# First layer norm by ScalarE's square root and one Newton step; GELU split on ScalarE; matmuls and loads reordered at the border and in the last slot

## The reference

```python
xn = _layernorm(x, axis=-1)              # (x - m) / sqrt(v + 1e-5)
...
local_out = _full_attention(x, local_qkv_w, scale)
sparse_out = _sparse_global_attention(x, sparse_qkv_w, scale)   # keeps the 102 largest scores of a row
mem_out = _memory_head(x, memory_bank, memory_proj_w, mem_out_w, mem_out_b)
pred_out = _prediction_head(x, ...)      # two linear layers, exact GELU, a third layer
...
return combined @ warboss_w + warboss_b
...
g = _silu(_L0_ffn_ref(xn, ...))          # relu(xn @ w1 + b1) @ w2 + b2, width 2048
x = x + s * g
```

## Time and profile before

| | |
|---|---|
| Time, median of 3 runs | 2529.58 us (2529.27 to 2530.76) |
| The profiled execution: its own time | 2529.44 us |
| The profiled execution: span from the first to the last instruction | 2527.6 us |
| PE busy | 2515.6 us |
| PEld busy | 2120.0 us |
| DVE busy | 2291.1 us |
| ACT busy | 1299.4 us |
| POOL busy | 1151.8 us |
| DMA | 551.74 MB, mean 218 GB/s |

### The profile page before, as it was taken

How to read it: one execution, slowest core, us unless ns; L and a number is a source line. 1 busy time by engine, 2 the same in 40 slices (tenths; PEclk the granted TensorE clock), 3 DMA queues, 4 the chain that set the end, 5 groups by cost and what they waited for, 6 DMA issues and landing times.

```text
span 2527.6 us, 36088 instructions
## 1 busy us (share of the span) xinstructions
PE 2515.6 (100%) x12432; PEld 2120.0 (84%) x12432; DVE 2291.1 (91%) x5184; ACT 1299.4 (51%) x2128; POOL 1151.8 (46%) x975
## 2 busy tenths in 40 slices
PE   9999999999999999999999999999999999999999
PEld 8888888878888888888888888888888888888887
DVE  7566556999999999999999999999999999999995
ACT  5666666644444444444544444444444444444443
POOL 2544444533444444444444444444444444444444
PEclk9999999999999999999999999999999999999999
DMA  8888888964655565546554665466556654665443
GB/s 262 331 309 314 309 311 326 340 230 138 236 197 200 167 234 200 200 167 233 200 200 166 224 206 197 166 219 214 200 167 216 215 199 164 216 217 199 165 157 122
DMA packets 166149, 551.74 MB, mean 218 GB/s; under 512 B 17936, under 2 KB 32976, under 8 KB 157648
## 3 DMA queue, kind: packets, MB, share of 16 engines
q1 hardware_dynamic: 165680, 548.90, 61.9%
q10 hardware_dynamic: 288, 0.52, 0.1%
HBM read 415.15 MB, written 134.22 MB: 217 GB/s over the span
## 4 chain that ended last, share of the span: by engine, by line
PE 95%; DVE 4%; ACT 0%; issue 0%; POOL 0%; POOLq 0%; ACTq 0%
PE acc L74 9%; PE acc L76 9%; PE acc L75 9%; PE hid L76 9%; PE hid L74 9%; PE hid L75 9%; PE ps L74 5%; PE ps L76 5%; PE ps L75 5%; PE o L1709 4%; PE scores L1696 4%; PE o L1713 2%; PE scores L74 2%; PE scores L76 2%; PE scores L75 2%; PE o L75 2%
## 5 line engine op out<-in xcount | busy, mean ns | idle before, releaser
L1428 POOL TENSOR_TENSOR h_lo<-h,h_hi 128x512 fp32r<-128x512 f32 x254 | 336.0, 1323 | 719.7 <-ACT h_hi L1323 718.2
L1561 DVE MAX8 ranks<-early 128x8 f32<-128x512 f32 x819 | 564.7, 689 | 13.0
L1581 DVE MATCH_REPLACE8 early<-ranks,early 128x512 f32<-128x512 f32 x756 | 511.1, 676 | 0.0
L1322 ACT ACTIVATE h<-hid,small 128x512 f32<-128x512 f32 x255 | 175.7, 689 | 479.9 <-PE hid L76 479.8
L74 PE MATMUL acc<-w,h_hi 128*128 128x512 f32 x1016 | 408.0, 402 | 0.0
L76 PE MATMUL hid<-xnT,w 128*128 128x512 f32 x1020 | 397.5, 390 | 0.0
L74 PE MATMUL hid<-xnT,w 128*128 128x512 f32 x1020 | 397.0, 389 | 0.0
L75 PE MATMUL hid<-xnT,w 128*128 128x512 f32 x1020 | 396.8, 389 | 0.0
L76 PE MATMUL acc<-w,h_lo 128*128 128x512 f32 x1016 | 396.5, 390 | 0.0
L75 PE MATMUL acc<-w,h_hi 128*128 128x512 f32 x1016 | 396.5, 390 | 0.0
L1428 POOL TENSOR_TENSOR pT_s<-pT,pT_s 128x512 fp32r<-128x512 f32 x256 | 327.2, 1300 | 42.2 <-ACT pT_s L1337 42.2
(11 more groups left out here) (237 smaller groups left out, 5170.2 us busy)
## 6 DMA issues: line engine op xcount, KB each, us to landing
w<-ffn_scratch SPq DMA_DIRECT2D x512, 512.0 KB, 4.1
xnT_scratch<-xnT SPq DMA_DIRECT2D x16, 2048.0 KB, 13.7
kv_scratch<-kv_out SPq DMA_DIRECT2D x32, 1024.0 KB, 6.1
tl<-tile_scratch SPq DMA_DIRECT2D x64, 512.0 KB, 4.0
tile_scratch<-tiles_out SPq DMA_DIRECT2D x15, 2048.0 KB, 8.5
xnT<-xnT_scratch SPq DMA_DIRECT2D x60, 512.0 KB, 7.1
ffn_scratch<-ffn SPq DMA_DIRECT2D x16, 1024.0 KB, 4.3
values<-kv_scratch SPq DMA_DIRECT2D x16, 1024.0 KB, 6.2
```

What stands on the lines that cost most here:

```text
L1322: nc.scalar.activation(h32[:, c % 2, :], src[:, :], ACT.Relu, bias=bias)
L1428: return nc.gpsimd.tensor_tensor(out_, value, hi_.bitcast(F32), ALU.subtract).then_inc(ready, 1)
L1561: l_step = count(nc.vector.max(top_l[:, own], larger[:, :]))
L1581: l_step = count(nc.vector.match_replace(larger[:, :], top_l[:, own], larger[:, :], LOWEST))
```

## The change

- **First layer norm.** For half 0, ACT computes the square root of var + eps (`ACT.Sqrt`) as soon as DVE has it, DVE takes its reciprocal and makes one Newton step instead of seed and three steps. The other halves are as before.
- **First projections.** All high parts of mp and pi come first (8 matmuls), then the 8 with the weights' low parts, which alone wait for `w_first`. ACT copies the weights of only one block of rows, not two, ahead of the transposed tokens. `WARM` is 48 instead of 60.
- **GELU, in every half.** ACT writes GELU back into the PSUM bank, waits for its own result, and copies the high part from there; DVE's cast is gone, and its two low parts (128x512 each) are taken from PSUM. The banks of p1a and p1b are free only when those are made.
- **Border.** On PE, `f2` of chunk 0 goes ahead of the local scores of slot 1, `f2` of chunk 1 ahead of the transposes behind them, and in slot 2 `f2` of chunk 4 ahead of the first transposes of the sparse head. `full_max` and `full_inverse` of slot 3 come one round earlier. SP loads w2's chunk 2 and w1's chunk 4 earlier.
- **Last slot.** The parts of `f2` for tile 0 are each moved ahead by one place.

The core of the diff:

```diff
-WARM = 60
+WARM = 48
...
+            act.wait_ge(ln_step, LN_VAR)
+            nc.scalar.activation(rstd[:, :], var[:, :], ACT.Sqrt).then_inc(deviation, 1)
             act.wait_ge(mp_in, 32)
             nc.scalar.activation(wp_hi[:, :, 0:2 * P], wp[:, :, 0:2 * P], ACT.Copy).then_inc(w_h, 1)
-            for k in (0, 1):
-                weights(k)
+            weights(0)
             for k in range(KT):
                 tokens(k)
-            for k in (2, 3):
+            for k in (1, 2, 3):
                 weights(k)
...
                             c = int(name == "p1b")
-                            last = nc.scalar.activation(gelu[:, c, :], src, ACT.Gelu, bias=b_p1[:, c:c + 1])
+                            nc.scalar.activation(src, src, ACT.Gelu, bias=b_p1[:, c:c + 1]).then_inc(gelu_step, 1)
+                            act.wait_ge(gelu_step, 2 * n + c + 1)
+                            last = nc.scalar.activation(gelu_hi[:, c, :], src, ACT.Copy)
...
-                link(nc.vector.tensor_scalar(rstd[:, :].bitcast(I32), var[:, :].bitcast(I32),
-                                             -0.5, RSQRT_SEED, ALU.mult, ALU.add))
-                link(nc.vector.tensor_scalar(var[:, :], var[:, :], -0.5, None, ALU.mult))
-                for _ in range(NEWTON):
+                if first(n):
+                    nc.vector.tensor_scalar(half_var[:, :], var[:, :], -0.5, None, ALU.mult)
+                    dve.wait_ge(deviation, 1)
+                    link(nc.vector.reciprocal(rstd[:, :], rstd[:, :]))
+                    var_scaled, steps = half_var, 1
...
-                    dve.wait_ge(bank_read, done(n, "p1b"))
-                    nc.vector.tensor_copy(gelu_hi[:, :, :], gelu[:, :, :]).then_inc(ghi_ready, 1)
-                    dve.wait_ge(ghi_ready, n + 1)
-                    subtract(gelu_lo[:, :, :], gelu[:, :, :], gelu_hi[:, :, :]).then_inc(lo_ready, 1)
+                    for c, name in enumerate(("p1a", "p1b")):
+                        dve.wait_ge(bank_read, done(n, name))
+                        subtract(gelu_lo[:, c, :], ps[:, bank(n, name), :], gelu_hi[:, c, :]).then_inc(lo_ready, 1)
...
+        FIRST_ROUNDS = {1: (1, 2), 3: (2, 3)}
...
-                r_max, r_inverse = (1, 2) if m == 1 else (R_MAX[T % HTILES], R_INVERSE[T % HTILES])
+                r_max, r_inverse = FIRST_ROUNDS.get(m, (R_MAX[T % HTILES], R_INVERSE[T % HTILES]))
...
                     load_kv(U_VL, 0)
+                    load_w2(2, 2)
                     load_tl(2, 2, 2)
-                    load_w2(2, 2)
+                    load_w1(4, 4)
                     load_w2(3, 3)
...
             transposes(2)
             f2(C, c, h, (0,))
             f1(C + 2, c + 2, h)
+            f2(C + 1, c + 1, h, (0,))
             pe.wait_ge(mix_ready, m - 2)
             head_out(g, U_VS)
             f1(C + 3, c + 3, h)
-            f2(C + 1, c + 1, h, (0,))
+            f2(C + 2, c + 2, h, (0,))
             pe.wait_ge(at_l, g + 1)
             mix(m - 2, (m - 2) % TL_RING)
-            for i in (2, 3):
-                f2(C + i, c + i, h, (0,))
+            f2(C + 3, c + 3, h, (0,))
```

More of the change, by code:

```diff
@@ L244, in stage1 @@
     CONSTS = 3
+    LN_VAR = 3
     with ExitStack() as ctx:
@@ L699, in layer_norm_parts @@
                 link(nc.vector.tensor_scalar(var[:, :], mv[:, :, 1], EPS, None, ALU.add))
-                link(nc.vector.tensor_scalar(rstd[:, :].bitcast(I32), var[:, :].bitcast(I32),
-                                             -0.5, RSQRT_SEED, ALU.mult, ALU.add))
-                link(nc.vector.tensor_scalar(var[:, :], var[:, :], -0.5, None, ALU.mult))
-                for _ in range(NEWTON):
+                if first(n):
[3 more added lines that the diff above has]
+                    var_scaled, steps = half_var, 1
+                else:
+                    link(nc.vector.tensor_scalar(rstd[:, :].bitcast(I32), var[:, :].bitcast(I32),
+                                                 -0.5, RSQRT_SEED, ALU.mult, ALU.add))
+                    link(nc.vector.tensor_scalar(var[:, :], var[:, :], -0.5, None, ALU.mult))
+                    var_scaled, steps = var, NEWTON
+                for _ in range(steps):
                     link(nc.vector.tensor_tensor(nt[:, :], rstd[:, :], rstd[:, :], ALU.mult))
-                    link(nc.vector.tensor_tensor(nt[:, :], nt[:, :], var[:, :], ALU.mult))
+                    link(nc.vector.tensor_tensor(nt[:, :], nt[:, :], var_scaled[:, :], ALU.mult))
                     link(nc.vector.scalar_tensor_tensor(out=rstd[:, :], in0=nt[:, :], scalar=1.5, in1=rstd[:, :],
@@ L920, in first_projections @@
                 dst = [ps[:, bank(0, name), :] for name in ("mp", "pi")]
+                pe.wait_ge(w_h, 1)
                 for k in range(KT):
                     pe.wait_ge(bank_read, k + 1)
-                    if k == 0:
-                        pe.wait_ge(w_first, 1)
                     for d, m in zip(dst, (MP, PI)):
-                        c = slice(m * P, (m + 1) * P)
-                        nc.tensor.matmul(d, wp_hi[:, k, c], xnT[:, 0, k, HI, :], start=k == 0, stop=False)
-                        nc.tensor.matmul(d, wp_lo[:, k, c], xnT[:, 0, k, HI, :], start=False, stop=False)
+                        nc.tensor.matmul(d, wp_hi[:, k, m * P:(m + 1) * P], xnT[:, 0, k, HI, :],
+                                         start=k == 0, stop=False)
+                pe.wait_ge(w_first, 1)
+                for d, m in zip(dst, (MP, PI)):
+                    for k in range(KT):
+                        nc.tensor.matmul(d, wp_lo[:, k, m * P:(m + 1) * P], xnT[:, 0, k, HI, :],
+                                         start=False, stop=False)
                 for d, m in zip(dst, (MP, PI)):
@@ L1280, in slot @@
                     finished()
-                load_w1(C + 4, c + 4)
+                if m > 1:
+                    load_w1(C + 4, c + 4)
                 if T == 0 and b < B:
@@ L1765, in slot @@
                 if T % 2 == 0:
+                    if m == 2:
+                        f2(C, c, h)
                     pe.wait_ge(pT_h, 4 * g + 2)
@@ L1769, in slot @@
                     transposes(2)
-                    f2(C, c, h)
+                    if m > 2:
+                        f2(C, c, h)
                     f1(C + 2, c + 2, h)
@@ L1787, in slot @@
                 else:
+                    if m == 1:
+                        f2(C, c, h)
                     pe.wait_ge(pT_h, 4 * g + 2)
                     head_scores(T % TL_RING, T_QL, U_KL, sl_done)
-                    f2(C, c, h)
+                    if m > 1:
+                        f2(C, c, h)
                     if not known_first(m, 2):
@@ L1796, in slot @@
                     f1(C + 2, c + 2, h)
+                    if m == 1:
+                        f2(C + 1, c + 1, h)
                     pe.wait_ge(pl_ready, m + 1)
                     transposes(0)
-                    f2(C + 1, c + 1, h)
+                    if m > 1:
+                        f2(C + 1, c + 1, h)
                     f1(C + 3, c + 3, h)
```

10 lines of the change are left out of this document (6 added, 4 removed).

## The result

The changed kernel takes 2534.80 us (median of 22 runs), the kernel before 2530.06 in the runs beside it: ratio 1.0017, 95% interval 1.0012 to 1.0023. That is 4.7 us more, where the forecast was 2.1 us above the profiled execution's time (2531.5 us) and 2533.8 was the upper end of the range. The sign and the class (within 0.2%) hold, the size doesn't. The profiled execution took 2534.98 us, its span is 2532.4, 4.8 more than before.

A forecast was written before the change was run, and what follows sets the result against it. PE was taken as the bound, so only its waits could be won. Half 0 +1.5, border +0.6, last slot 0: +2.1 on the profiled 2529.44 gives 2531.5 us; range 2528.3 to 2533.8, the forecast's own bounds 2529.7 to 2533.8.

The forecast's parts named there:

- First layer norm: Half 0, var + eps to scaling: 1.35 us instead of 2.38, a gain of 1.03 us (0.7 to 1.2).
- ACT's chain to mo: Half 0: start 1.03 us earlier, table load 1.28 and GELU pair 1.25 more; mo at 40.5 instead of 39.02.
- the rival with 1.4 us more for the switch: Table load ahead of Exp in half 0 takes 1.4 us longer than the trace's 1.28: 2532.9 us, chance 0.04.
- Waits 2.8 us: Half 0: PE waits 2.8 us ahead of mo, for the low part of wt.
- Half 0: Half 0 costs 1.5 us (1.0 to 2.2) instead of gaining 1.3, and all that follows is later by it.
- Halves 1 to 15: ACT has 1.25 us more work in each half, but 1.2 us remain ahead of p2: costed at nothing.
- Slot 1: Border: local scores 1.83 us later, PE waits 1.7 us for w2; the slot ends 1.2 us later than before.
- Slots 2 to 7: PE at +0.2 in slot 2, leaves slot 3's wait 0.7 us earlier, is 0.6 us later from slot 7 on.
- the border's term: Slots 1 to 7 together cost +0.6 us (-1.1 to +1.7); PE not waiting in slot 7 would fell it.
- Last slot: Wait of 0.4 us is covered, but the last f2 part needs POOL's last low part: nothing won or lost.
- the two terms: The costs of half 0, +1.5 us (1.0 to 2.2), and of the border, +0.6 us (-1.1 to +1.7).

The follow-up runs named there:

- e4: Changed kernel with 24 more transposes of the identity on PE ahead of mo in half 0, result unread: ratio 1.0012 to the kernel before, median 2533.06 us.
- e2: Changed kernel with the GELU path of the kernel before (GELU into SBUF, DVE makes high and low part): ratio 1.0008 to the kernel before, median 2532.06 us.
- e3: Changed kernel with one tiny Exp in half 0 while ACT waits for DVE's maximum, loading the table early: ratio 1.0009 to the kernel before, median 2532.57 us.
- e1: Changed kernel with the first layer norm of the kernel before, without ScalarE's square root: ratio 1.0007 to the kernel before, median 2531.69 us.
- e5: Changed kernel with six more DVE instructions at the start, one subtraction done in seven slices: ratio 1.0013 to the kernel before, median 2533.43 us.
- e8: Changed kernel with Exp's table loaded early, GELU path and slot 1's order as before, six more DVE instructions: ratio 0.9991 to the kernel before, median 2527.82 us.
- e10: Changed kernel with Exp's table early, GELU path and whole border as before, six more DVE instructions: ratio 0.9997 to the kernel before, median 2529.10 us.
- e11: e8 with DVE's mix in slot 3 at round 5 instead of 7 of its search: ratio 0.9998 to the kernel before, median 2529.96 us.
- e12: e8 measured once more, unchanged: ratio 0.9992 to the kernel before, median 2528.08 us.
- e6: Changed kernel with slot 1's order on PE as in the kernel before: ratio 1.0011 to the kernel before, median 2533.00 us.
- e7: Changed kernel with Exp's table loaded early, GELU path and slot 1's order as before: ratio 0.9999 to the kernel before, median 2529.75 us.
- e9: Kernel before with only the new first layer norm (square root, one Newton step, six DVE instructions fewer): ratio 1.0009 to the kernel before, median 2531.97 us.

## Why the prediction was off

- **First layer norm**: forecast -1.03, measured -1.33 at the scaling (8.74 against 10.07), 0.19 of it because the input landed earlier; 1.24 us from var to the scaling, 1.35 forecast. The new order of the first projections and the shorter warm-up gave 0.14 more.
- **ACT's chain to mo**: load +1.28 and pair +1.22 (1.25 forecast). Right. mo came at 40.00 and not at 40.5 through the step above. The load took the trace's 1.28 and Exp began 0.01 us behind it, so the rival with 1.4 us more for the switch falls.
- **What the wait ahead of mo costs**: here the prediction failed. "Waits 2.8 us" was taken as the whole price. The wait was 2.8 (2.72 shown), and behind it PE ran at half its clock: 1.6 us more, 1.45 net in half 1, which nothing in the sum stood for. Half 0 cost 2.4, not 1.5. The Trainium skill (TensorE: Matmul & The Clock Gate, "What's actually happening") says that the clock depends on how busy PE has been; rows at 0.50 here, and e4, agree.
- **Halves 1 to 15**: nothing, as forecast. In half 1 gelu's low part is ready at 64.45 and p2 starts at 65.72: 1.27 to spare, 1.2 forecast.
- **Slot 1**: right in every step. Local scores 1.86 behind (1.83 forecast), the wait for w2 1.63, of which 1.47 are shown (1.7), the transposes 3.5 behind the half's lag (3.5).
- **Slots 2 to 7**: the sum right by luck (+0.74 at slot 5, 0.6 forecast), the way wrong. I had PE leave slot 3 0.7 early and pay at slots 5 and 7. It left it 1.3 early and paid in the same slot, 1.75 us for DVE's mix, a wait that I hadn't looked for. DVE still waited 0.77 at slot 5, and PE not at all in slot 7, which by the prediction's own sign fells the border's term as it was argued.
- **Last slot**: nothing, as forecast; the wait only changed place (POOL's low part ends at 2514.94, PE goes on at 2515.00).
- **Stage 2 in the middle**: the second failure. The sum had no term behind slot 7; the layer norm's six instructions fewer were counted for their time in the first 10 us only. They cost 2.1 us in slot 30.
- **The range**: the bounds of the two terms, +1.0 to +2.2 and -1.1 to +1.7, add up to 2529.3 to 2533.3 us; the 2529.7 to 2533.8 given as the forecast's own bounds don't follow from them. The measured 2534.8 lies outside either.

In PE's lag: -1.5 + 2.5 + 1.45 - 0.2 (won back in half 14) = 2.3; 0.7 in the border, 0.2 won back in slot 23, where the kernel before pays for its own hole at 1183.86, 2.1 in slot 30: 4.9, and the spans differ by 4.8. Without the two missing terms (3.55) it would have been 1.3.

## What to carry to other kernels

An idle time of the bounding engine is not priced by its length alone: behind 2 to 3 us of waiting it may run slowly for 3 us more, so here several short waits (e2) were cheaper than a long one, and filler work on PE can pay (e4). Where DVE and POOL both read two SBUF operands in a loop with a margin of 0.1 to 0.2 us between their starts, a shift of 0.2 us anywhere can cost 2; list the starts of both before changing the phase of either, and if a change that should be local costs time far away, look for the first step of 1.8 instead of 0.7 us. A ScalarE table can be loaded for nothing by one tiny activation in an idle time ahead of the need (e3).

## What the runs showed of the hardware

- DVE has a hole of 0.23 instead of 0.04 us between two dependent steps at places set by the number of DVE instructions ahead: at 1183.86 and 1627.96 in the kernel before, at 1410.91 and 1856.89 with six instructions fewer. Busy times of the engines between the two holes, of the kernel before and of the changed one:

```profile
1183.86:1627.96 444.10, 444.06 (x2123) 371.31 (x2122) 434.72 (x980) 216.24 (x336) 206.68 (x182) 1.00 0.58 198
```

```profile
1410.91:1856.89 445.98, 444.36 (x2122) 371.23 (x2121) 436.63 (x980) 216.33 (x336) 206.56 (x182) 1.00 0.59 202
```

  In both, DVE works off 980 instructions. All kernels run here keep to one of the two patterns by their count (e1, e5, e8, e10, e11 and e12 to the first; e2, e3, e4, e6, e7 and e9 to the second). Six instructions fewer do not move the hole by six: counted in the profile's DVE instructions it stands behind 2287 and 3267 in the first pattern, and behind 2774 and 3754 in the second. What makes the hole is not shown. A rival that no run tests is the fetching of instructions: the traces have such packets, one of 8 KB 0.7 to 3.4 us behind each of the four holes (at 1187.21, 1630.40, 1411.57 and 1857.68), but over 70 more of them stand at no visible hole.
- A DVE step of 128x512 with both inputs in SBUF that starts 0.03 to 0.52 us behind the start of POOL's 1.3 us subtraction takes 1.82 to 1.32 us instead of 0.68, and ends 0.55 us behind POOL's; where DVE starts first, POOL's takes up to 1.68. DVE's mix step, with one input in PSUM, starts during work of POOL 47 times in the changed kernel and takes 0.67 to 0.69. All seven kernels with the hole near 1409 have the pair of 1.8 and 1.5 us behind it, and none of the seven others has it there.
- From half 0 on, all five waits of PE over 2 us were followed by a granted clock of 0.50 for 3.4 us: 2.72 (changed kernel), 2.90 and 2.50 (e5), 2.71 (e6) and 2.07 (e1, slot 1). Of the four waits between 1.93 and 1.98 one was (e10, slot 3, 1.95) and three were not (kernel before 1.96, e3 1.98, e9 1.93). None under 1.8 was. Why the waits near 1.95 differ stays open.
